# An expert loop whose vector engine evicts before it adds in, and whose row gathers run four tiles ahead instead of eight

## What is computed

```python
hn2 = _layernorm(x, ln2_g, ln2_b).reshape(-1, h)          # 2048 tokens of 128
idx = jnp.argmax(hn2 @ gate_w + gate_b, axis=-1)          # one of 8 experts for each token
mid = jax.nn.relu(jnp.einsum('th,ehf->etf', hn2, w1) + b1[:, None, :])   # F = 512
y = jnp.einsum('etf,efh->eth', mid, w2) + b2[:, None, :]
return x + y[idx, jnp.arange(hn2.shape[0])].reshape(b, s, h)
```

## Time and profile before

| | us |
|---|---|
| median of 3 runs | 686.66 (685.08, 686.66, 688.59) |
| the profiled execution | 691.15 |
| its span, first to last instruction | 689.4 |

### The profile page before, as it was taken

The page is one execution under the profiler, slowest core; times in us unless marked ns, Lnnn a source line. Parts: engine busy times, 40 slices in busy tenths (PEclk is TensorE's granted clock), DMA queues, the critical chain, the costliest instruction groups (busy, mean ns, idle before and its releaser), DMA issues.

```text
span 689.4 us, 15329 instructions
## 1 busy us (share of the span) xinstructions
PE 590.4 (86%) x5153; PEld 398.7 (58%) x5157; DVE 489.0 (71%) x1214; ACT 391.4 (57%) x828; POOL 216.0 (31%) x372
## 2 busy tenths in 40 slices
PE   5989789999985699577689999888989999855995
PEld 3756245656545499455356556555546665453995
DVE  5576968888866377479756677687867888663675
ACT  2647057777761265227456677776777777611552
POOL 4902900000000625303434334454222321006244
PEclk9988789999996699879899999999999999966899
DMA  3175773344004210202763433535333640042101
GB/s 97 3 233 146 159 191 70 87 96 99 4 2 123 84 41 32 66 27 82 195 178 71 90 82 77 132 78 137 72 97 83 146 96 5 2 123 84 41 28 36
DMA packets 56469, 60.23 MB, mean 87 GB/s; under 512 B 10121, under 2 KB 48937, under 8 KB 53225
## 3 DMA queue, kind: packets, MB, share of 16 engines
q1 hardware_dynamic: 52968, 52.56, 31.1%
q0 software_dynamic: 2560, 6.30, 3.0%
q10 hardware_dynamic: 864, 0.39, 0.2%
HBM read 39.96 MB, written 18.87 MB: 85 GB/s over the span
## 4 chain that ended last, share of the span: by engine, by line
PE 58%; DVE 14%; issue 7%; ACT 7%; DMA 6%; DVEq 3%; POOL 3%; another core or an unknown queue 1%; SPq 1%; ACTq 0%; POOLq 0%
PE bank L790 13%; PE bank L757 10%; PE bank L728 8%; PE bank L806 3%; DMA QS<-MT 3%; PE bank L741 3%; PE bank L1338 2%; PE bank L315 2%; DMA KS<-k_parts 2%; PE bank L820 2%; ACT PR L886 2%; DVE PR L1459 2%; PE bank L1327 2%; PE bank L743 1%; PE bank L320 1%
## 5 line engine op out<-in xcount | busy, mean ns | idle before, releaser
L886 ACT ACTIVATE PR<-bank 128x512 f32<-128x512 f32 (+1 forms) x384 | 208.2, 562 | 108.4 <-PE bank L757 98.4
L962 DVE TENSOR_REDUCE MN<-bank 128x2 f32<-128x512 f32 x256 | 167.8, 687 | 46.1 <-PE bank L728 44.6
L757 PE MATMUL bank<-QS,KS 128*128 128x256 bf16 (+1 forms) x768 | 140.7, 266 | 14.0 <-ACT PR L886 10.1
L790 PE MATMUL bank<-PR,VP 128*32 128x256 f32 (+1 forms) x1536 | 116.6, 376 | 2.5 <-POOL PR L1047 1.8
L728 PE MATMUL bank<-KS,QS 126*128 126x256 bf16 x512 | 101.3, 280 | 5.6 <-DVE MN L962 5.2
L757 PEld LDWEIGHTS bank<-QS,KS 128*128 128x128 bf16 x768 | 69.9, 99 | 39.1 <-ACT PR L886 20.3
L949 DVE TENSOR_REDUCE MN<-bank 128x2 f32<-128x512 f32 (+1 forms) x96 | 64.3, 687 | 37.8 <-PE bank L743 37.1
L728 PEld LDWEIGHTS bank<-KS,QS 126*128 126x128 bf16 x512 | 43.0, 104 | 39.8 <-DVE MN L962 22.0
L1058 POOL COPY VP<-UV 128x64 f32<-128x64 f32 x64 | 15.0, 240 | 157.5 <-PE bank L790 157.5
L1327 PE MATMUL bank<-PR 128*128 128x128 f32 x368 | 53.6, 289 | 6.6 <-issue 6.2
L1338 PE MATMUL bank<-W,PR 128*128 x368 | 54.5, 293 | 4.6 <-issue 2.8
(11 more groups left out here) (279 smaller groups left out, 952.3 us busy)
## 6 DMA issues: line engine op xcount, KB each, us to landing
QS<-q_parts SPq DMA_DIRECT2D x66, 192.0 KB
KS<-k_parts SPq DMA_DIRECT2D x66, 192.0 KB
q_parts<-QP SPq DMA_DIRECT2D x24, 192.0 KB, 4.7
k_parts<-KP SPq DMA_DIRECT2D x10, 384.0 KB, 4.9
q_parts<-QP SPq DMA_DIRECT2D x24, 128.0 KB, 4.5
W<-in_w SPq DMA_DIRECT2D x1, 2048.0 KB, 12.7
hat_rows<-X SPq DMA_DIRECT2D x8, 256.0 KB, 3.3
hat_rows<-HAT SPq DMA_DIRECT2D x8, 256.0 KB, 3.7
```

Source lines behind the costliest of these rows:

```text
L757: last = pe.matmul(d, KS[:, bass.ds(slot_of(b) + n * S + kt * P, P)], QS[:, bass.ds(slot_of(b) + n * S + lo, S - lo)], start=True, stop=True)
L790: last = pe.matmul(bank[4 if q < 2 else 7][32 * j:32 * j + 32, lo:S], VP[:, (kt * H + h) * 32:(kt * H + h + 1) * 32], PR[:, (n % 8) * CH + ...
L886: act.activation(PR[:, (n % 8) * CH:(n % 8) * CH + w], bank[2 + n % 2][:, 0:w], ACT.Exp, scale=HEAD_SCALE).then_inc(s["exped"], 1)
L962: dve.tensor_reduce(out=o, in_=bank[n % 2][:, :].rearrange("p (t k) -> p t k", k=S), axis=AX_X, op=ALU.max, negate=True).then_inc(s["maxed ...
```

## The change

Three things are edited. `AHEAD` goes from 8 to 4. On DVE the tile number of place k - 3 is still read after the copy of the weights, but then the eviction of place k - 2 comes, and the add-in of place k - 3 after it; since two evicted places now stand unread, `NY` goes from 2 to 3, which also shifts `W1S` and `MIDT` by 128 columns within `PR`. At step k = 23 DVE reads two tile numbers ahead of its eviction and adds in two places behind it; the last place of all is always of tile 15, and is added in without a register.

```diff
-NY = 2
+NY = 3
-AHEAD = 8
+AHEAD = 4
@@
-            def add_own(i):
-                tau = dve.value_load(TAU[0:1, i:i + 1], min_val=0, max_val=NT - 1)
+            def tile_reg(i):
+                return dve.value_load(TAU[0:1, i:i + 1], min_val=0, max_val=NT - 1)
+
+            def add_own(i, tau):
+
                 dve.wait_ge(s["out"], i + 1)
                 at_least(dve, s["y"], i)
-                row = UV[:, bass.ds(tau * (2 * P) + P, P)]
+                row = YROW[NT - 1] if tau is None else UV[:, bass.ds(tau * (2 * P) + P, P)]
@@
-                if k >= 3:
-                    add_own(k - 3)
+                if 3 <= k <= NR:
+                    tau = tile_reg(k - 3)
+                if k == NR:
+                    next_tau = tile_reg(k - 2)
                 if k >= 2:
                     evict(k - 2)
-            add_own(NR - 1)
+                if 3 <= k <= NR:
+                    add_own(k - 3, tau)
+                if k == NR:
+                    add_own(k - 2, next_tau)
+            add_own(NR - 1, None)
```

## The result

The changed kernel takes 677.27 us (median of 4 runs, 672.68 to 679.43) against 686.53 us before; the ratio is 0.9865, with a 95% interval of 0.9824 to 0.9907. That is 9.3 us less, give or take 2.9. The profiled execution took 678.15 us, its span is 676.4 us, against 689.4.

What follows compares the result with a forecast made beforehand. DVE's queue, 1.97 us a place, was the bound, with PE right behind. Profiled: 691.15 - 8.4 (shorter train) + 1.1 (turn ends) = 683.9 us; timed median taken as 680.5, between 679.4 and 681.9; range 675 to 688.5.

Steps and rivals of the forecast that it cites:

- The bound and the loss: Even places bound by DVE's queue at 1.97 us; 14.9 us lost at both turns' starts while gathers ran at 1.25 us.
- The shorter train: Start of each turn: AHEAD = 4 makes the train four gathers shorter, so stalls end sooner; 6.6 to 10.2 us gained, 8.4 taken.
- rival (b): Start of turns: fewer gathers behind PE's burst end the stall altogether, up to 14.9 us less, say 675 us; chance 0.12.
- a loss to the clock: After the stalls, PE's half clock lost 1.3 and 2.3 us; these 3.6 us might stay lost after the shorter stall.
- The middle: Even places: eviction ahead of add-in changes nothing, zero taken; upper bound 2.8 us gained from PE's bubble.
- Rival (c): Loop: gathers there cost 0.3 us each, eight more run there; with the stall unchanged, 690.2 us, slower; chance 0.08.
- The end of the turns: Last scatters wait for add-in 20, now behind eviction 21: 0.4 and 0.7 us later, +1.1 us taken, 0 as lower end.
- The discount for timed runs: Median 4.5 us below the profiled execution; if all that is the stall's, timed runs hold only 70% of the 14.9 us.
- The longer gather beside a copy: Loop: four more gathers of each turn could take 0.25 us longer beside DVE's copy, covered by 5 us; nothing in the sum.

Runs made afterwards that it cites:

- one gather for each place: Lead-by-table kernel with its wait table changed to one gather per place in the loop, none paired except 5 and 6; median 676.39 us, 0.985 of before over six runs.

## Why the prediction held, point by point

**The bound and the loss: right.** Of the 14.9 us lost at the start of the turns the change takes 11.6 away, and one gather for each place 13.7: most of the loss is the train's. Its end sets the end of the stall (leads of 4, 6, 8 and 16); the length of PE's burst has no part in it.

**The shorter train: right in mechanism, too small in size.** Gather 7 was to start about 3 us behind gather 6, and starts 2.69 and 3.14 us behind it. Place 0 to 6 was to take 13.7 to 15.1 and 14.6 to 16.9 us; it took 14.01 and 12.96. The term was 6.6 to 10.2, taken as 8.4; it measured 4.34 + 7.26 = 11.6, outside its own bounds, and 78% of the 14.9 us lost, which is the size that rival (b) named, though not by its sign: a stall was left.

The 3.2 us too little have two parts. I let the stall end when the train had landed, 3.1 to 3.2 us behind gather 6; place 1 started 2.27 and 2.40 us behind it, which is 1.6 us for both turns (less 0.3, as places 1 to 6 took 20.0 us together and not 19.7). And I took half of a loss to the clock, 1.8 us of 3.6; in turn 1 the clock stayed up, and in turn 2 it was up again when the even places began. A third shift moved the turns but not their sum: PE ran at half clock during place 0's product in turn 1 before and in turn 2 after, so that place 0 came 7.17 and then 6.22 us behind gather 0 in turn 1, and 6.04 and then 6.96 in turn 2. Kernels with the same code up to there show both values, so that is chance. Without it turn 1 would have come out at 13.1, below its range as well: that it stayed inside is luck.

**The middle: right, but for 0.2 us.** Zero forecast; places 6 to 22 took 0.2 and 0.03 us more, and 0.4 and 0.1 with the lead alone. The last gather was to meet the first scatters "at no cost": in turn 1 gather 15 at 248.47 and the first scatter at 249.73 stand 1.26 us apart, and place 10 to 11 took 2.15 us beside them in place of 1.98. With a lead of three the same meeting cost 3 us. Rival (c) priced a gather in the loop at 0.3 us, partly from place 4 to 5 of turn 1, which takes 2.3 us or more in every kernel here, with gathers beside it or not.

The chain of waits of the changed kernel names PE in some even places,

```profile
243.18 0.96 PE bank L1338 x8
...
245.14 0.98 PE bank L1338 x8
```

and DVE's queue in others, 1.97 us apart at the weights' copy, as in the earlier trace rows:

```profile
256.46 0.06 DVEq L1459
...
258.43 0.06 DVEq L1459
```

So the new order didn't pass the bound from one to the other; the two stand as close as the earlier trace rows had it, and eight down records still take 0.96 us of the place, not the 0.89 of the up product.

**The end of the turns: half as dear.** I took +0.7 and +0.4, and it is +0.04 and +0.53. Scatter 13 starts 0.87 us behind eviction 21, as forecast (0.9), and POOL's pace does the rest. In turn 1 eviction 21 itself came sooner, 1.90 us behind the last bias in place of 2.53; why PE's signal took less was not tried.

**The discount for timed runs: its reason was wrong.** I put up to 30% of the stall down to the profiled execution, because it was 4.5 us over the median. But the kernel with DVE's order alone was profiled in an execution of 685.79 us, below the median, and its turns are as long (62.7 and 63.0 us). AHEAD = 16 costs 14.9 us in timed runs and 13.9 in the profiled turns. The timed gain of the change, 9.3 us against 10.8 in the turns, is smaller by less than its interval; so is that of the lead alone (9.5 against 12.2), and with AHEAD = 6 it is 4.7 against 6.9, so a smaller discount isn't ruled out. Without the discount the terms as measured give 686.66 - 11.6 + 0.6 + 0.2 = 675.9; the 677.3 measured is 1.4 us above that, inside the interval too. So the forecast of 680.5 missed by 3.2 us because of the term of the shorter train, which was too small by as much; the discount (1.1 too much time) and the end of the turns (0.5 too much) were made up for by the middle's 0.2 and these 1.4.

**The longer gather beside a copy: no cost, and rare.** A gather beside DVE's copy took 1.19 us in the earlier trace rows. The Trainium skill's page "SBUF — State Buffer", section "SBUF: two separate sides", says that GpSimd can't write descriptors during such a copy. The trace agrees for that row, but overlap alone isn't enough. In the changed kernel the nine gathers in turn 1's loop took 0.94 to 0.95 us, though five of them started while a copy was under way, 0.33 us or more behind its start, and three had one start with them or behind them. The long ones here started 0.06 to 0.10 us behind the start of a copy: the one in the earlier trace rows, and with the add-in first again two gathers of the kernel with one gather for each place (1.14 and 1.18 us). None of them moved a place.

## What to carry to other kernels

Indirect DMAs from GpSimd should not be let go as fast as they can be issued while other engines depend on TensorE's signals: here a short lead, with one gather for each step of the loop, was worth more than a deep one. Count the scatters in too, since what is put off at the start can meet them later and make the same train. And when all engines stop at once with nothing to wait for in the profile, look at what ran at an even beat through the stop, and what ended when it did.

## What the runs showed of the hardware

I had not expected that a few indirect DMAs hold TensorE up at all. While they followed one another at 1.25 us, PE did one record in 1.4 us in place of 0.11, and its signals reached DVE and ACT late, the last of them 2.3 to 3.7 us behind the start of the train's last gather (a wait of 11.2 us with sixteen), while DVE's signal to ACT passed in 0.03 us. This begins 7 to 9 us behind the first gather, and not always: with the lead alone one turn of seven gathers went through without it. At 1.8 us and more apart, sixteen did hardly any such thing. Half the bytes changed nothing, and neither did plain DMAs of 1.44 MB beside the gathers. Four in a row are enough when PE is at full work (place 11 to 12 with a lead of three), and so were three close behind others. Along which path GpSimd's DMAs reach PE is open: no run here separates the making of the descriptors from their reading by the DMA engines.
